# Order of TensorE's work in a mixture-of-experts attention: projection pieces and scores first, fp32 work behind them

## What is computed

```python
q = _rope(jnp.einsum('bsd,hdp->bhsp', x, Wq))
k = _rope(jnp.einsum('bsd,hdp->bhsp', x, Wk))
gv = _gate(x, Wsel_v)                                   # top 2 of 8 experts
v = jnp.einsum('bsd,bhse,hedp->bhsp', x, gv, Wv)
att = jax.nn.softmax(jnp.einsum('bhsp,bhtp->bhst', q, k) / np.sqrt(P), axis=-1)
o = jnp.einsum('bhst,bhtp->bhsp', att, v)
go = _gate(x, Wsel_o)
return jnp.einsum('bhsp,bhse,hepd->bsd', o, go, Wo)
```

## Time and profile before

| | us |
|---|---|
| median of 3 runs | 2860.67 (2857.79 to 2864.15) |
| profiled execution | 2874.2, span 2872.4 |
| PE matmul busy | 2439.6 (85%), mean granted clock 0.878 |
| DVE busy | 1844.8 (64%) |
| ACT busy | 1277.2 (44%) |
| POOL busy | 1126.1 (39%) |
| the stage's first score to the last fold | 1414 to 2329 |

### The profile page before, as it was taken

The page is one execution under the profiler, slowest core; times in us unless marked ns, Lnnn a source line. Parts: engine busy times, 40 slices in busy tenths (PEclk is TensorE's granted clock), DMA queues, the critical chain, the costliest instruction groups (busy, mean ns, idle before and its releaser), DMA issues. The chain is left out here.

```text
span 2872.4 us, 42613 instructions
## 1 busy us (share of the span) xinstructions
PE 2439.6 (85%) x12238; PEld 1757.9 (61%) x12238; DVE 1844.8 (64%) x3912; ACT 1277.2 (44%) x2820; POOL 1126.1 (39%) x1322
## 2 busy tenths in 40 slices
PE   5999989667656999757699999999999975599788
PEld 3767667555555888536465656565566644489655
DVE  6544544666456888566578768777766645567688
ACT  4545554444224666423354444443444432244365
POOL 2000000154014999201476656666666600012288
PEclk7969788788668999976799999999999987699799
DMA  1000000041004666000234343432434320000074
GB/s 38 1 0 0 0 0 0 18 106 32 5 18 98 151 150 152 3 17 26 66 71 92 78 94 74 89 92 70 90 88 82 78 52 5 30 1 1 10 165 105
DMA packets 62992, 161.64 MB, mean 56 GB/s; under 512 B 7563, under 2 KB 18699, under 8 KB 55000
## 3 DMA queue, kind: packets, MB, share of 16 engines
q1 hardware_dynamic: 62792, 159.30, 24.5%
HBM read 156.26 MB, written 3.01 MB: 55 GB/s over the span
## 5 line engine op out<-in xcount | busy, mean ns | idle before, releaser
L1895 PE MATMUL bank<-l2h_og,l2h_wo 128*128 128x512 f32 x512 | 263.6, 599 | 12.6 <-DVE LNT L2139 11.6
L1997 ACT ACTIVATE l2h_pr<-twin,l2h_nmx 128x512 f32<-128x512 f32 x256 | 176.0, 688 | 173.3 <-PE bank L1884 121.2
L1989 ACT ACTIVATE l2h_prT<-bank 128x512 f32<-128x512 f32 x256 | 151.7, 592 | 210.1 <-PE bank L1884 210.1
L986 POOL TENSOR_TENSOR l1m_hid_lo<-l1m_hid,l1m_hid_hi 128x512 fp32r<-128x512 f32 x136 | 217.8, 1621 | 62.1 <-ACT l1m_hid_hi L965 61.4
L306 ACT ACTIVATE l0a_pr<-l0a_sc,l0a_nmx 128x128 f32<-128x128 f32 (+3 forms) x256 | 143.5, 561 | 196.1 <-DVE l0a_nmx L245 195.5
L367 PE MATMUL bank<-l0a_prT,l0a_v 128*128 128x128 f32 x1280 | 221.3, 311 | 6.5 <-DVE l0a_yT L271 6.5
L2142 DVE TENSOR_REDUCE l2h_nmx<-twin 128x2 f32<-128x1024 f32 x128 | 156.1, 1220 | 104.6 <-PE twin L1874 103.9
L2115 DVE TENSOR_TENSOR l2h_vg<-bank,l2h_gv 128x512 f32<-128x512 f32 x256 | 175.1, 684 | 54.5 <-POOL l2h_vs L2210 31.5
L367 PEld LDWEIGHTS bank<-l0a_prT,l0a_v 128*128 128x128 f32 x1280 | 201.8, 228 | 9.9 <-issue 9.9
L2210 POOL TENSOR_TENSOR l2h_vs<-l2h_vg 128x256 f32<-128x256 f32 x256 | 190.9, 746 | 28.1 <-DVE l2h_vg L2115 27.7
L78 POOL MEMSET l0x_k<- 128x154 f32 x1 | 0.2, 228 | 486.8 <-issue 486.8
(11 more groups left out here) (638 smaller groups left out, 6501.9 us busy)
## 6 DMA issues: line engine op xcount, KB each, us to landing
l2h_gt<-l2m_gate_rows SPq DMA_DIRECT2D x128, 512.0 KB, 6.9
l1m_c<-l1m_weights SPq DMA_DIRECT2D x64, 512.0 KB, 6.3
l3m_c<-l3m_weights SPq DMA_DIRECT2D x32, 512.0 KB, 6.5
l0m_c<-l0m_weights SPq DMA_DIRECT2D x16, 512.0 KB, 6.8
l1m_w<-in_l1m_pairs SPq DMA_DIRECT2D x32, 192.0 KB, 6.1
l2h_fresh<-in_l2m_wqkv SPq DMA_DIRECT2D x8, 768.0 KB, 5.1
l2h_wo<-in_l2m_wo SPq DMA_DIRECT2D x8, 512.0 KB, 4.9
l0m_w<-in_l0m_pairs SPq DMA_DIRECT2D x8, 192.0 KB, 5.1
```

Source lines behind the costliest of these rows:

```text
L986: nc.gpsimd.tensor_tensor(hid_lo[:, at, :], hid[:, (n + PRE) % 4, :], hid_hi[:, at, :], ALU.subtract)\
L1895: nc.tensor.matmul(ybank[:, :], wo[s][:, e, :], og[:, e % 4, :], start=(e == 0), stop=(e == E - 1))\
L1989: nc.scalar.activation(prT[:, j // 2 % 2, h, :, j % 2 * P:(j % 2 + 1) * P], tbank[:, :].rearrange("p (c q) -> p c q", c=TPB), ACT.Copy).th ...
L1997: nc.scalar.activation(pr[:, h, :], sbank[:, h, :], ACT.Exp, bias=nmx[:, k % 2, h:h + 1], accum_out=rs[:, g % 2, t, h:h + 1]).then_inc(exp ...
```

## The change

In PE's step the three pieces of the next group stand first, then the score; the two turns, the two projections and the rest follow, without pieces between. In DVE's step the three takes stand first, ahead of the fold, the reduce, the reciprocal and the gate products; only the thirteenth piece's product stays behind the gate products. Buffers, banks, waits of each instruction, and the lists of ACT, POOL and SP stay as they are.

```diff
@@ -1923,22 +1923,18 @@
                     def step(it, k, last):
                         pieces = pieces_at(k, last)
                         q = k - TURN_GATES
+                        for g, n in pieces:
+                            make(it, g, n, last)
                         if due(k, 0, last):
                             score(it, k)
                         if due(k, 1, last):
                             if 1 <= q <= B and not last:
                                 pe.wait_ge(go_copied, it * B + B + q)
                             turn_probs(it, k - 1, 0)
-                        for g, n in pieces[0:1]:
-                            make(it, g, n, last)
                         if due(k, YLAG, last):
                             project(it, (k - YLAG) // TPB, (k - YLAG) % TPB * 2)
-                        for g, n in pieces[1:2]:
-                            make(it, g, n, last)
                         if due(k, 1, last):
                             turn_probs(it, k - 1, 1)
-                        for g, n in pieces[2:3]:
-                            make(it, g, n, last)
                         if due(k, YLAG, last):
                             project(it, (k - YLAG) // TPB, (k - YLAG) % TPB * 2 + 1)
                         if due(k, 3, last) and k % 2 == 1:
@@ -2130,6 +2126,8 @@
                     def step(it, k, last):
                         pieces = pieces_at(k, last)
                         gates_due = due(k, OLAG, last)
+                        for g, n in pieces:
+                            take(it, g, n, last)
                         if due(k, YLAG + TPB, last) and k % TPB == (YLAG + TPB) % TPB:
                             g = (k - YLAG - TPB) // TPB
                             dve.wait_ge(y_done, it * GROUPS * E + (g + 1) * E)
@@ -2146,15 +2144,11 @@
                             dve.wait_ge(expd, it * 2 * TILES + 2 * k)
                             sums = rs[:, g % 2, :, :]
                             nc.vector.reciprocal(sums, sums).then_inc(inverted, 1)
-                        for g, n in pieces[0:1]:
-                            take(it, g, n, last)
                         if gates_due:
                             gate(it, (k - OLAG) // TPB, (k - OLAG) % TPB * 2, last)
-                        for g, n in pieces[1:2]:
-                            take(it, g, n, last)
                         if gates_due:
                             gate(it, (k - OLAG) // TPB, (k - OLAG) % TPB * 2 + 1, last)
-                        for g, n in pieces[2:3] + factor_at(k, last):
+                        for g, n in factor_at(k, last):
                             take(it, g, n, last)
```

## The result

The changed kernel takes 3016.78 us (median of 4 runs, 2999.34 to 3026.10) against 2862.41 (4 runs, 2857.79 to 2871.76) of the kernel before: 1.0504 times as long, interval 1.0466 to 1.0542, so 133 to 155 us more. The forecast was 136 more, 2997. The profiled execution took 3026.1, its span 3024.3, at a mean granted clock of 0.875 (0.878 before).

The account below looks back on a forecast made before the run. The prediction took the stage to be PE-bound, with nothing removed from PE's list and waits added. Terms of 103 + 4 + 9 + 20 = 136 us on 2860.7 gave 2997 us, range 2930 to 3038.

Parts of the forecast that it names:

- clean increments: Stage steps 8 to 123 without special work: 3.56 us more per group of four, 29 groups, 103 us.
- first eight steps: The stage's first eight steps, which have no projection: about 4 us more.
- (e): Picks on DVE at t = 1 (k mod 4) stand ahead of the takes: 14 us, less 5, net 9.
- (f): POOL's weight splits at k = 39 and k = 22 delay its sums: together 20 us, bounds 5 and 35.
- (a): PE's third piece waits for DVE to free one of two PSUM banks: 0.44 us in 124 steps, 55 us.
- (b): PE's second turn waits for ACT's copy of the first: 0.15 us, bounds 0 to 0.25 a step.
- (c): At t = 1 (k mod 4), DVE's late factor product holds the next second piece: 1.11 us, (a) and (b) included.
- (d): At t = 3 (k mod 4), DVE's take waits for POOL's sum, delaying fold and projection: 1.29 us with (a).
- rivals 2 and 3: Faster by hidden weight loads, 2834 us, chance 0.03; quicker fp32r streaming offset by bank waits, about 2900, chance 0.01.
- Rival 1: Only (a) and perhaps (b) cost time, POOL and ACT being early enough: 55 to 70 us, about 2925, chance 0.17.
- Rival 4: PE was waiting anyway where the third piece now waits, so no change: 2861 us, chance 0.03.
- Rival 5: DVE's late takes and POOL's backlog meet: (d) also at t = 0 and 2, twice (f), about 3045, chance 0.13.

Follow-up runs that it names:

- E1: Changed kernel with PE's first turn moved between the second and third piece; ratio 1.0453 to the kernel before.
- E9: Changed kernel with PE's second projection ahead of the second turn; 3030.62 us, run one time.
- E4: Changed kernel with the thirteenth piece (factor) ahead of the weighing on PE, its product waiting for the weighing; ratio 1.0525 to the kernel before.
- E5: Changed kernel with first turn between pieces, DVE's fold first, POOL's sums first and factor ahead of the weighing; ratio 1.0140 to the kernel before.
- E2: Changed kernel with DVE's fold into LNT ahead of the three takes; ratio 1.0362 to the kernel before.
- E3: Changed kernel with POOL's sums ahead of its qk split and weight split; ratio 1.0340 to the kernel before.
- E8: Changed kernel with the first turn between second and third piece and POOL's sums ahead of its splits; ratio 1.0288 to the kernel before.

## Why the prediction was right, and where it was not

In the stage the change costs what was forecast, in the main by the mechanisms forecast. The whole difference is larger, 154 by the medians and 151.9 by the spans, against 136: the rest lies in equal code ahead of and behind the stage. No run shows whether any of it is the change's, as the start of the stage moves by up to 33 us between the profiled executions. Measured against the terms, in us over the stage:

| term | forecast | measured |
|---|---|---|
| clean increments, 29 groups | 103 | 103 (29 x 3.55) |
| first eight steps, and pieces ahead of the first score | 4 | 13.2 (9.3 and 3.9) |
| (e) picks, beyond the clean increments | 9 | 8.5 |
| (f) split at k = 39, three turns | 14.7 | 21.7 |
| (f) split at k = 22 and 23, beyond the clean increments | 1.9 | 1.4 |
| (f) split in the first turn | 3 | within the first eight steps |
| steps with turned gates, beyond the clean increments | 0 | 2.2 |
| loop's return, beyond the clean increments | 0 | -11.6 (6.0 idle, 5.6 the step behind) |
| k = 123, where no pieces are left (7.61 to 6.41), and rounding | 0 | -2.0 |
| sum | 135.6, with (f) rounded up 136 | 136.4 |

**(a), the ring.** Right in its place and its price. The take starts 0.44 behind the third matmul where 0.52 was taken, so the wait is 0.36 to 0.44; E1 takes it away, and (b) with it, and the steps at t = 0 and 2 go back to their old length; E9 takes (b) alone, 0.11, which leaves 0.35 at t = 0 and 0.45 at t = 2 for the ring.

**(b), ACT's copy.** Forecast 0.15. The second turn starts 0.95 to 1.02 (timeline of after, t = 0 and 1) behind the projection's start instead of 0.86, so 0.09 to 0.16; E9 gets 0.11 from its place.

**(c), the product at t = 1.** Forecast 1.11, measured 1.17. E4 moved it and gained 0.50 there; what is left of it in E5 is 0.27.

**(d), the head of the line at t = 3.** Forecast 1.29, measured 1.36. E2 (the fold moved out) and E3 (the block taken away) each remove a part, and by what the prediction named: the queue on DVE and the order on POOL.

**What the reorder removes.** Nothing, as taken. The step at t = 0 above has the fp32 work in one run: from first turn to projection 0.49 (0.50 taken) and from second turn to projection 0.46 (0.44 taken), so no load is hidden that wasn't. The pieces' matmuls start 0.23 apart in the run of six as before. That refutes rivals 2 and 3, the hidden loads and the streaming rate. E5, with most of the waits gone, agrees: its group is 0.61 longer than before, not shorter. Rival 1, the ring alone, asked for 8.6 and 8.1 at t = 1 and 3 and fell by 9.37 and 8.96. Rival 4, no effect, fell by the ratio. Rival 5 foresaw (d) at t = 0 and 2 too, which stayed at 6.2 and 6.3; its other half, the clock, did come, at k = 39 and around k = 22, but not for twice the cost. PE's busy share in the stage was to be near 88%; it is 91% (926.80 of 1023 us, 1430:2453).

**Where it was wrong.** That the sum comes out to 0.4 us is luck: misses cancel, and with the loop's return as it was the stage would have lost 148. Term (f) was mis-sized at k = 39: 4.9 a turn, measured 7.2. The longer wait is 4.84, as forecast, and what was left out is that behind it PE runs at 1.2 GHz for a stretch; the cooling had been put into the bounds (35) and not into the value. The first eight steps stood at 4 in the sum and 3 in (f), and cost 13.2; of that 3.9 are the three pieces that now lie ahead of the first score, which the prediction left out. Steps with turned gates were at nothing and cost 2.2. The loop's return was no term at all and gave 11.6 back: 6.0 of idle time, whose cause is open, and 5.6 in the steps behind it, which had run at a granted clock of 0.50 and now run at 1.00.

**Where the expectations of the experiments were wrong.** E1, E4 and E9 each removed the wait that they aimed at, by the amount expected, and were expected to keep it; in all three t = 3 rose by 0.45 to 0.87. The prediction had computed POOL's lateness at t = 3 as 0.47 and so had the number that says that no slack is left: time taken out between the weighing at t = 1 and the fold at t = 3 is met by POOL, and in E1 by the lost cover too. The rise in E4 and E9 is larger than the gain (0.87 against 0.50 and 0.11) because each edit also makes POOL's sum later, by way of the weighing in E4 and of ACT in E9. Besides, E2 was to bring t = 3 to 8.1 to 8.3 and brought 8.44, and E3 was to take 4 us a turn off the two steps at k = 22 and took next to nothing.

## What to carry to other kernels

A ring of two buffers works only while other work of the producer stands between its uses: count from the start of a buffer's last write through the consumer's start to the producer's next start (0.44 + 0.74 = 1.18 here, against the 0.92 that one piece between gives, 0.23 + 0.69) before pulling uses together. On an engine that works in order, put an operation that can block behind those that others wait for. And judge the gain of taking one wait away by the next near-bound: four edits brought a group from 30.80 to 27.86 together, and alone one 0.62 and one less than nothing. The only kernel faster than both came from neither order but in a step that was already late in the profile before: a 3.5 us operation moved to where its engine had slack.

## What the runs showed of the hardware

A wait of 5.3 us on PE at k = 39 cost 7.2 us on average of three: behind it stands a granted clock of 0.50, and the fp32 projection takes 2.07 instead of 1.12. Shorter waits had a stretch at 0.50 behind them too: 3.09 at k = 54, and 2.39 in the kernel before. The clean steps, in which PE or its loads wait 0.4 to 1.2 us at a time, have 1.00.

The idle time at a loop's return depends on the order of the code around it: 4.6 to 5.6 us with PE's steps as before and 1.8 to 3.4 as after the change. Neither a smaller load nor other instructions first at the top changed it. Such a return can cost more than its idle time: before, 4.95 and 5.59 of idle and 5.6 more in the two steps behind, at a granted clock of 0.50; after, 2.22 and 2.34 with the clock at 1.00. In E1 and E8, whose first return has 2.43 and 2.09 of idle, a stretch at 0.50 still stands behind it (1768:1770 and 1729:1731).

Equal code ahead of the stage took between 1356.5 and 1389.5 us in the twelve profiled executions. So a difference between two single spans of up to some 30 us is no evidence of anything here, but the score-to-score times of clean steps repeat to some 0.02.
